# Gathers of a graph kernel packed by edge rank and kept in HBM, from where SP loads the padded tiles

## The reference, cut to what matters

```
layer 0, 3 rounds:  agg = segment_sum(norm[:, None] * out[src], dst);  out = clip(0.9 * agg + 0.1 * y, 0, 1)
layer 1:  w_e = (relu(e_feat @ en1_w.T + en1_b) @ en2_w.T + en2_b).reshape(-1, 32, 32)
layer 1, 6 rounds:  msg = einsum('ei,eio->eo', out[src], w_e);  agg = segment_sum(msg, dst) + conv_bias;  out = h = gru(relu(agg), h)
layer 2, 1 round:   agg = segment_sum(h[src], dst);  out = relu((agg * norm_dst) @ weight + bias)
layer 3, 1 round:   out = segment_sum(ew[:, None] * x[src], dst), self loops added
```

## Time and profile before

| What | Value |
|---|---|
| median of 3 runs | 34976.55 us (34972.99 to 34978.08) |
| the profiled execution's own time | 34982.19 us |
| its span, first to last instruction | 34980.4 us |
| busy: PE, DVE, ACT, POOL | 59%, 30%, 30%, 65% of the span |
| gathers (L613) in all | 21824, 946 ns each |

### The profile page before, as it was taken

One profiled execution on the slowest core, in us unless ns is written; L12 is line 12 of the kernel. 1 busy time (PEld: TensorE's weight loads), 2 busy tenths in 40 slices (PEclk: granted clock), 3 DMA queues, 4 the chain that ended last, 5 costly groups with the idle time before them and its releaser, 6 DMA issues. The chain is left out here.

```text
span 34980.4 us, 467404 instructions
## 1 busy us (share of the span) xinstructions
PE 20562.4 (59%) x139128; PEld 8821.7 (25%) x139128; DVE 10599.1 (30%) x15910; ACT 10358.5 (30%) x27640; POOL 22641.0 (65%) x23430
## 2 busy tenths in 40 slices
PE   5557110110110799899999989989998996111111
PEld 3333100100100233333333333333333332000000
DVE  7665000000000344344444434434443442000000
ACT  0004100000000355455445545545554553000000
POOL 6880676677677566566556656647665664775775
PEclk8779555555555899999999999999999998555555
DMA  2115114113112322522522242252243224114014
GB/s 64 23 23 190 21 15 14 19 15 14 19 15 14 51 61 61 51 61 61 53 59 60 60 52 60 61 51 62 61 59 54 60 61 40 15 15 17 15 15 17
DMA packets 2058079, 1520.36 MB, mean 43 GB/s; under 512 B 1419487, under 2 KB 1801927, under 8 KB 2054464
## 3 DMA queue, kind: packets, MB, share of 16 engines
q0 software_dynamic: 749568, 390.42, 16.8%
q1 hardware_dynamic: 878380, 953.21, 9.1%
q10 hardware_dynamic: 430032, 175.29, 1.9%
HBM read 1250.48 MB, written 253.52 MB: 43 GB/s over the span
## 5 line engine op out<-in xcount | busy, mean ns | idle before, releaser
L613 POOL DMA_INDIRECT sb_xs<-node_rows,sb_idx x21824 | 20655.1, 946 | 11479.6 <-issue 6504.6
L713 PE MATMUL banks<-sb_spread,sb_eh_sb 128*128 128x512 f32 x23808 | 11923.9, 624 | 202.9 <-DVE sb_spread L668 169.5
L668 DVE TENSOR_TENSOR sb_spread<-sb_xs,banks_p 128x2048 f32<-128x2048 f32 x2976 | 6793.5, 2287 | 9479.0 <-PE banks L713 8282.7
L778 ACT ACTIVATE sb_g<-banks 128x512 f32<-128x512 f32 x11904 | 6962.7, 596 | 6043.9 <-PE banks L713 6008.2
L693 PE MATMUL banks_s<-sb_mask,sb_xs 128*32 128x16 f32 x43648 | 990.7, 202 | 10714.5 <-DMA sb_xs<-node_rows,sb_idx 10714.0
L772 ACT ACTIVATE sb_s<-banks_s 32x32 f32<-32x32 f32 x10912 | 2048.3, 188 | 12201.0 <-PE banks_s L693 11924.7
L713 PEld LDWEIGHTS banks<-sb_spread,sb_eh_sb 128*128 128x128 f32 x23808 | 4072.3, 190 | 5020.9 <-issue 4325.7
L650 DVE TENSOR_TENSOR sb_mask<-sb_meta_t,sb_node 128x128 f32<-128x128 f32 x2728 | 789.9, 290 | 11950.7 <-PE banks_s L693 11862.4
L701 PE MATMUL banks_p<-sb_g,sb_en 128*32 128x256 f32 x47616 | 3814.4, 393 | 3.9 <-ACT sb_pj L787 3.9
L693 PEld LDWEIGHTS banks_s<-sb_mask,sb_xs 128*32 128x32 f32 x43648 | 719.1, 128 | 10955.4 <-issue 10333.5
L271 POOL DMA_INDIRECT slots<-sb_rows,sb_slot_u x1600 | 1985.1, 1241 | 700.4 <-issue 696.8
(11 more groups left out here) (183 smaller groups left out, 8703.3 us busy)
## 6 DMA issues: line engine op xcount, KB each, us to landing
sb_eh_sb<-eh SPq DMA_DIRECT2D x1488, 512.0 KB
sb_xs<-node_rows,sb_idx POOLq DMA_INDIRECT x21824, 2.3
eh<-sb_eh_sb ACTq DMA_DIRECT2D x248, 512.0 KB, 3.2
sb_idx<-sb_src_t SPq DMA_DIRECT2D x2728, 4.0 KB, 1.7
parts<-sb_part ACTq DMA_DIRECT2D x2728, 16.0 KB, 1.4
sb_g<-parts SPq DMA_DIRECT2D x44, 992.0 KB
slots<-sb_zeros SPq DMA_DIRECT2D x16, 2294.0 KB, 45.8
sb_rowin<-slots SPq DMA_DIRECT2D x248, 148.0 KB, 3.3
```

Source lines behind the costliest of these rows:

```text
L613: nc.gpsimd.indirect_dma_start(m.xs[h][:, t * D:(t + 1) * D], None, m.node_dram, bass.IndirectOffsetOnAxis(ap=m.idx[h][:, t:t + 1], axis=0 ...
L668: V.tensor_tensor(m.spread[q], m.xs[h].rearrange("s (t i) -> s t i", i=D)[:, tiles, :].unsqueeze(3) .broadcast_to([P, TS, D, WN]), m.mask_ ...
L713: mm(m.ps_g[:, t % 4, :], m.eh[h][:, t * K:(t + 1) * K], m.spread[t // TS][:, t % TS, :, :], start=True, stop=True).then_inc(g_done, 1)
L778: nc.scalar.activation(m.g[h // 2][:, :, (h % 2) * TC + t, :], m.ps_g[:, t % 4, :].rearrange("k (i n) -> k i n", n=WN), copy).then_inc(g_s ...
```

## The change

Gathers no longer follow the padded tiles but the edges' ranks. Edge k (in the order of windows) is slot k mod 128 of packed tile k div 128, so 200000 edges take 1563 packed tiles; JT = 1568 of them are gathered, in JBODIES = 49 bodies, 196 batches. A padded tile keeps its place in `owner`, in `eh` and in the results, but its edges now stand in the partitions that their rank gives. Two windows that share a packed tile have each a padded tile that loads the same 128 rows; the mask takes each window's own.

POOL gathers packed batch n into `xg[h]`, and SP stores it to `xg_dram` in HBM (`keep`). For padded batch n SP reads eight tile numbers from the table `row_at` into registers (`rows_of_batch`) and loads eight packed tiles from `xg_dram` to `xs[h]` (`fetch`). A padded tile's number is never below that of the packed tile it needs, so batch n can be loaded as soon as gathers 0 to n are kept. SP's program staggers the three by a batch: index load n, store n-1, loads n-2. After 49 bodies SP goes on with the loads alone for the 13 that are left. `place_windows` works out the tables, and the new phase `close_up_sources` moves the source numbers from padded to packed tiles with matmuls.

```diff
 TC, L, BODIES = 8, 4, 62
 TP = L * TC * BODIES
+JBODIES = 49
+JT = L * TC * JBODIES
...
+def rows_of_batch(nc, m, i, h):
+    table = bass.at_runtime_partition(m.row_at[0:1, h * TC:(h + 1) * TC], i)
+    _, rows = nc.values_load_multi_w_load_instructions(
+        table, engines=[mybir.EngineType.SP], min_val=0, max_val=JT - 1,
+        skip_runtime_bounds_check_because="place_windows keeps every number between 0 and JT - 1")
+    return rows
...
         @block.gpsimd
         def _(pool):
-            with pool.Fori(0, BODIES) as i:
+            for i in peeled(pool, JBODIES):
                 for h in range(L):
-                    n = i * L + h
                     pool.wait_ge(idx_in[h], i * 16 + 16)
-                    pool.wait_ge(summed, n + 1)
-                    if edge_matrices:
-                        pool.wait_ge(made, 2 * n + 2)
+                    wait_after_first(pool, put[h], i * 16)
                     hold(pool, held_pool)
                     for t in range(TC):
                         nc.gpsimd.indirect_dma_start(
-                            m.xs[h][:, t * D:(t + 1) * D], None, m.node_dram,
-                            bass.IndirectOffsetOnAxis(ap=m.idx[h][:, t:t + 1], axis=0)).then_inc(gathered[h], 16)
+                            m.xg[h][:, t * D:(t + 1) * D], None, m.node_dram,
+                            bass.IndirectOffsetOnAxis(ap=m.idx[h][:, t:t + 1], axis=0)).then_inc(got[h], 16)
...
         @block.sync
         def _(sp):
-            for i in peeled(sp, BODIES):
+            def prefetch(i, n, h):
+                wait_after_first(sp, got[h], i * GT)
+                hold(sp, held_sp)
+                sp.dma_start(m.idx[h], m.src_c[:, bass.ds(n * TC, TC)]).then_inc(idx_in[h], 16)
+            def keep(i, n, h):
+                sp.wait_ge(got[h], i * GT + GT)
+                hold(sp, held_sp)
+                sp.dma_start(m.xg_dram[:, bass.ds(n * TC * D, TC * D)], m.xg[h]).then_inc(put[h], 16)
+            def fetch(i, n, h):
+                rows = rows_of_batch(nc, m, i, h)
+                sp.wait_ge(summed, n + 1)
+                if edge_matrices:
+                    sp.wait_ge(made, 2 * n + 2)
+                hold(sp, held_sp)
+                for t in range(TC):
+                    sp.dma_start(m.xs[h][:, t * D:(t + 1) * D],
+                                 m.xg_dram[:, bass.ds(rows[t] * D, D)]).then_inc(gathered[h], 16)
+                if edge_matrices:
+                    sp.wait_ge(g_done, n * TC + TC)
+                    hold(sp, held_sp)
+                    sp.dma_start(m.eh[h], m.eh_dram[:, bass.ds(n * TC * K, TC * K)]).then_inc(eh_in[h], 16)
+            def kept_and_fetch(i, n, h):
+                sp.wait_ge(put[h], i * 16 + 16)
+                hold(sp, held_sp)
+                fetch(i, n, h)
+            skewed(sp, (prefetch, 0), (keep, 1), (kept_and_fetch, 2), bodies=JBODIES)
+            with sp.Fori(JBODIES, BODIES) as i:
                 for h in range(L):
-                    n = i * L + h
-                    wait_after_first(sp, gathered[h], i * GT)
-                    hold(sp, held_sp)
-                    sp.dma_start(m.idx[h], m.src_t[:, bass.ds(n * TC, TC)]).then_inc(idx_in[h], 16)
-                    if edge_matrices:
-                        sp.wait_ge(g_done, n * TC + TC)
-                        hold(sp, held_sp)
-                        sp.dma_start(m.eh[h], m.eh_dram[:, bass.ds(n * TC * K, TC * K)]).then_inc(eh_in[h], 16)
+                    fetch(i, i * L + h, h)
...
+def close_up_sources(nc, m):
...
+            for ch in range(OC):
...
+                for b in range(4):
+                    mm = nc.tensor.matmul(m.ps_g[:, b, 0:JT // 4], m.src_turned[ch % 2],
+                                          m.into[ch % 2][:, b * (JT // 4):(b + 1) * (JT // 4)],
+                                          start=(ch == 0), stop=(ch == OC - 1))
+                mm.then_inc(summed, 1)
```

More of the change, by code:

```diff
@@ L51 @@
 REST = NODES - FULL * NM
-assert EQ * ET == EDGES and TP >= EDGES // P + NW and OQ * OC == TP and NW >= NQ * NC
+assert EQ * ET == EDGES and TP >= EDGES // P + NW and JT * P >= EDGES and JT % 4 == 0 and OQ * OC == TP and NW >= NQ * NC
 @contextmanager
@@ L215, in place_windows @@
 def place_windows(nc, m):
-    with phase(nc, "placed") as (block, placed):
+    with phase(nc, "placed", "numbered", "kept") as (block, placed, numbered, kept):
         @block.vector
@@ L221, in _ @@
             V = nc.vector
[L222 to L226 removed]
+            do(V.tensor_copy(m.tiles[:, :], m.cnt[:, :]))
             a, b = m.tiles, m.scan0
@@ L233, in _, with tile_number @@
                 shift *= 2
-            do(V.tensor_tensor(m.first[:, :], a[:, :], m.tiles[:, :], ALU.subtract))
-            do(V.tensor_scalar_mul(m.first_slot[:, :], m.first[:, :], float(P)))
+            do(V.tensor_tensor(m.first_slot[:, :], a[:, :], m.cnt[:, :], ALU.subtract))
+            def tile_number(out, edges, more):
+                do(V.tensor_scalar_add(out[:, :], edges[:, :], float(more)))
+                do(V.tensor_copy(m.cnt_i[:, :], out[:, :]))
+                do(V.tensor_scalar(m.cnt_i[:, :], m.cnt_i[:, :], 7, None, ALU.logical_shift_right))
+                do(V.tensor_copy(out[:, :], m.cnt_i[:, :]))
+                do(V.tensor_tensor(out[:, :], out[:, :], m.iota[:, :], ALU.add))
+            tile_number(m.first, m.first_slot, 0)
+            tile_number(m.cnt, a, P - 1)
             for c in range(OC):
@@ L289, in place @@
                 if step > 0:
-                    dve.wait_ge(own, n * 6 + step + 1)
+                    dve.wait_ge(own, n * 7 + step + 1)
                 if step == 0:
@@ L304, in place @@
                 elif step == 5:
+                    V.tensor_tensor(m.slot_tf, m.slot_tf, m.win_now[h], ALU.add).then_inc(own, 1)
+                elif step == 6:
                     wait_after_first(dve, scattered[h], i * 16 * ST)
@@ L337, in _ @@
                             accum_out=m.slot_f[h][:, t:t + 1]).then_inc(slot_read, 1)
-                        if 1 <= t <= 7 and not (is_first(i) and h == 0):
+                        if 1 <= t <= 8 and not (is_first(i) and h == 0):
                             place(t - 1, i if h == 1 else i - 1, half - 1, 1 - h)
-            for step in range(7):
+            for step in range(8):
                 place(step, SBODIES - 1, 2 * SBODIES - 1, 1)
@@ L424, in unpack @@
                 rows = m.rowin[h].rearrange("s (t r) -> s t r", r=ROW)
-                V.tensor_copy(m.src_t[:, bass.ds(n * TC, TC)].bitcast(F32), rows[:, :, 0])
+                V.tensor_copy(m.src_t[:, bass.ds(n * TC, TC)],
+                              m.rowin[h].bitcast(I32).rearrange("s (t r) -> s t r", r=ROW)[:, :, 0])
                 V.tensor_copy(m.meta_t[:, bass.ds(n * TC * 3, TC * 3)].rearrange("s (t r) -> s t r", r=3),
@@ L575, in edge_pass @@
     GT = 16 * TC
-    with phase(nc, "idx_a", "idx_b", "idx_c", "idx_d", "gath_a", "gath_b", "gath_c", "gath_d",
+    with phase(nc, "idx_a", "idx_b", "idx_c", "idx_d", "got_a", "got_b",
+               "got_c", "got_d", "put_a", "put_b", "put_c", "put_d", "gath_a", "gath_b", "gath_c", "gath_d",
                "eh_a", "eh_b", "eh_c", "eh_d", "st_a", "st_b", "st_c", "st_d", "masked", "made", "summed",
@@ L579, in edge_pass, with skewed @@
             block, *sems):
-        idx_in, gathered, eh_in, stored = sems[0:4], sems[4:8], sems[8:12], sems[12:16]
-        masked, made, summed, g_done, g_sb, s_sb, grouped, pj_sb, folded, out_sb, held_sp, held_pool = sems[16:28]
-        twinned = sems[28]
-        def skewed(eng, *steps, tail=None):
-            for i in peeled(eng, BODIES, ahead=2):
+        idx_in, got, put, gathered, eh_in, stored = (sems[4 * k:4 * k + 4] for k in range(6))
+        masked, made, summed, g_done, g_sb, s_sb, grouped, pj_sb, folded, out_sb, held_sp, held_pool = sems[24:36]
+        twinned = sems[36]
+        def skewed(eng, *steps, tail=None, bodies=BODIES):
+            for i in peeled(eng, bodies, ahead=2):
                 for h in range(L):
@@ L1262, in build @@
             encode_edges(nc, m)
+            close_up_sources(nc, m)
             node_degrees(nc, m)
```

74 lines of the change are left out of this document (65 added, 9 removed).

## The result

The changed kernel takes 33343.36 us (median of 4 runs, 33337.04 to 33351.37) where the kernel before takes 34974.94 beside it: a ratio of 0.9534, 95% interval 0.9517 to 0.9550, 1632 us less. The forecast of 34,225 us had the sign and a little under half of the size.

What follows compares the result with a forecast made beforehand. Before, POOL's gathers bound light passes and DVE's spreads heavy ones; SP's loop would take over. Light -911, heavy +72 and setup +85 make -754 from 34982.2: 34228, so 34,225 us with the 5.6 lower median; range 33,300 to 35,450.

Steps and rivals of the forecast that it cites:

- the size of r: SP's block per padded batch, table read plus eight row loads: 5.8 us, between 4.3 and 6.7.
- I take 1.4: SP's table read of eight registers: 1.4 us, between nothing (hidden in waits) and 1.7.
- A row load: 0.55 us: SP's issue time for each of the eight row loads per batch: 0.55 us, low 0.54, high 0.63.
- SP's loop: Index load n+2 needs gather n, so two batches per loop: light 7.6 + r/2 = 10.5 us, heavy 8.45 + r/2 = 11.35.
- The formulas: Light pass 195 p + 46 + 54 r = 2407 us; heavy pass 636 + 195 x 11.35 = 2849 us.
- Rival A: POOL keeps the bound, r under 5: light pass 2266, heavy 2802, 33,235 us in all; chance 0.20.
- Rival B: SP's loop becomes the bound everywhere, slower from r = 6.36 on; 35,430 us at r = 6.7; chance 0.33.
- The hot rows: Zero-filled padding slots at a pass's end read one HBM row repeatedly; gathers land after 22.8 us in place of 2.3.
- A heavy pass: Longer filling, then batches of 11.35 us: 2849 against 2837 us, +12 a pass, six times +72.
- Setup: Closing up sources 40 plus 10 us, place_windows 10 plus 25: sum +85 us, high 150.
- Lies under POOL: The added DVE step in the setup's scatter, 100 x 0.1 us, was taken to be hidden under POOL.
- the threshold of 4.96: The r in us from which SP's two-batch loop, not POOL's 10.08 us a batch, decides light passes.

Runs made afterwards that it cites:

- experiment 5: Changed kernel with three more row loads per padded batch into a spare tile nobody reads: 35333.88 us, 1.0102 of the kernel before.
- experiment 1: Kernel before with each empty slot's source set to its own partition's number, so padding gathers 128 different rows: 34193.78 us, ratio 0.9774.
- experiment 3: Changed kernel with one load of eight fixed tiles per batch in place of table read and eight row loads: 32407.97 us, 0.9263 of the kernel before.
- experiment 7: Kernel before with only the eighth DVE step added to the scatter, its sum unused: first to last scatter 2521.2 us against 2471.1.
- the three reads: Changed kernel with the table read written three times a batch, though its trace holds it once: 33341.11 us, 0.9532 of the kernel before.

## Why the forecast was off, step by step

*The step that failed* is the size of r: "I take 1.4: nearer the upper end, since SP needs the eight values before the first address", and, less so, "A row load: 0.55 us". The read is 0.73 us, and a load 0.52 from start to start, so r is 4.9 us and not 5.8. With it failed what the forecast built on r, that SP's loop sets the pace of the light passes at 10.5 us with POOL waiting for the index load: POOL runs at its own 9.99 there, waits for index loads for 1.8 us in a pass, and pays 16 pauses of 1.2 us that the forecast did not have.

The Trainium skill's floor of about 600 ns for such a read ("DMA: Bandwidth & Descriptors", "Latency and other measured facts") is near the median of 726 ns of this trace, and its shortest, 533 ns, lies a little under that floor. The 200 ns a register of the Trainium skill ("Runtime: NRT & Kernel Launch", "Instruction fetch mechanics"), 1.6 us for eight, are said of registers loaded from HBM; the table `row_at` lies in SBUF, so no run here tests them.

*The formulas, with r = 4.9 in them,* give a light pass 195 x 10.08 + 46 + 54 x 4.9 = 2276 us (2265 measured), a heavy one 636 + 195 x 11.11 = 2802 (2813), and in all 34,977 - 1565 - 207 + 85 = 33,290 us; 33,343 measured. So the size of r takes the forecast from 34,225 to 33,290. The 53 us that are left are several misses that partly cancel: the light passes came out 11 us shorter each, the heavy ones 11 longer each, the setup 31 longer. That the batch fits so well (10.08 for 10.10) is luck: 10.08 was right for the kernel before (10.07 by the median), but in the changed kernel POOL's own pace is 9.99, and the pauses make up the rest. The loop itself shows in experiment 5, where r is large enough for it.

*Rival A*, POOL keeps the bound, asked for r under 5 and gave 33,235 and a light pass of 2266. It is what happened, 108 us off in the total. "The table read has to be nearly free" was too strong a condition: 0.73 us was enough. *Rival B* is real: its break-even of r = 6.36 lies near 6.1 on a straight line between the changed kernel and experiment 5, not quite three loads further on.

*The hot rows:* right in place, cause and size (experiment 1: 87 and 58 us for 89 and 62; the rows themselves, 13.9 less 11.11, give 67 for the 62).

*A heavy pass:* 11.15 a batch in place of 11.35 is -39 us, and the pass came out 36 below the forecast; the floor of 11.11 is more likely PE's than DVE's (experiment 3). The longer filling and the detour are paid: with cool padding the heavy pass before takes 2779, and the packed one is never under 2788.

*Setup:* forecast +85, measured +116: place_windows +25 for 35, closing up the sources +52 for 50, and the scatter +39 for 0 (experiment 7). "Lies under POOL" looked at DVE's time alone and not at what POOL does beside it.

## What to carry to other kernels

When two engines pass buffers in a ring, write the loop's time as (fixed part + r) over the batches in it, and look at the threshold above which it decides. Here a block of 4.9 us lay just under the threshold of 4.96; three more 16 KB transfers in it cost 6% and the whole gain, and a read moved ahead of a wait gave 0.6%. When the mean of a step agrees with a formula, look at the single steps too: here a mean of 10.10 us was 9.99 and a pause in every twelfth. Look at the addresses before the counts: half of the gain came from padding that no longer read one row, and one instruction in the setup gives it. A step that one engine can afford still shifts its neighbours; and an edit made for an experiment is to be counted in its trace, as the three reads show.

## What the runs showed of the hardware that was not expected

- A runtime HBM address costs SP little: loads with computed rows stand 0.517 us apart, with constant ones 0.474, and a TENSOR_LOAD of eight registers takes 0.54 us in the tail of a pass and 0.73 while gathers run.
- With gathers issued one behind the other, those of 128 equal rows land after 22.8 us, those of 128 different ones after 2.3, with the same bytes.
- Indirect gathers on POOL pause in every twelfth batch of eight, for up to 1.55 us, and less or not at all when their indices are there early; the cause is open.
- A scatter issue on POOL that starts under DVE's one-hot operations ends only with them, up to 2.8 us in place of 1.19.
- Chips differ: of the six on which experiments ran, three take 18% longer for the kernel before, all of it while gathers run, and there the same change has the other sign. On three the medians of before are 34,973 to 34,987 us, on the others 41,340 to 41,397.
